# Three edits to a fused attention, SSM and mixture-of-experts kernel: the SSM's first batch begun inside the first FFN, another order at the start, a finer end

## The reference

```python
# attention (one head over 128 features)
q, k, v = jnp.split(jnp.einsum('bse,he->bsh', x, w_qkv), 3, axis=-1)
probs = jax.nn.softmax(jnp.einsum('bqh,bkh->bqk', q, k) * scale, axis=-1)
out = jnp.einsum('bqk,bkh->bqh', probs, v)        # then w_proj, b_proj
# SSM
zxbcdt = jnp.einsum('bld,ed->ble', u, W_in)       # z, xBC, dt
dt = jax.nn.softplus(dt + dt_bias)
conv = conv_b                                     # 4 taps along the tokens
for w in range(4):
    conv = conv + xp[:, w:w + L, :] * conv_w[:, w]
xBC = jax.nn.silu(conv)                           # x, B, C
def step(h, inp):                                 # scan over the tokens
    h = h * dA_t[:, :, None, None] + jnp.einsum('bhp,bn->bhpn', dtx_t, B_t)
    y_t = jnp.einsum('bhpn,bn->bhp', h, C_t)
g = y * jax.nn.silu(z)                            # RMS norm, then W_out
# FFN: 16 experts, the best 4 of each token by a router (softmax of logits)
# per expert: swiglu(mlp1_w[e] @ t + b1) -> mlp2_w[e], weighted sum
```

## Time and profile before

| | |
|---|---|
| timed executions | 749.07, 747.16, 748.96 us |
| the profiled execution | 746.62 us, of it the span 744.9 us |
| PE busy | 712.4 us (96%) |
| DVE busy | 627.3 us (84%) |
| ACT busy | 577.0 us (77%) |
| GpSimd (POOL) busy | 239.7 us (32%) |
| first FFN on PE | about 124 to 320 us |
| SSM, with its first batch's projections | about 320 to 555 us |
| second FFN on PE | about 555 to 740 us |

### The profile page before, as it was taken

One profiled execution on the slowest core, in us unless ns is written; L12 is line 12 of the kernel. 1 busy time (PEld: TensorE's weight loads), 2 busy tenths in 40 slices (PEclk: granted clock), 3 DMA queues, 4 the chain that ended last, 5 costly groups with the idle time before them and its releaser, 6 DMA issues. The chain is left out here.

```text
span 744.9 us, 13019 instructions
## 1 busy us (share of the span) xinstructions
PE 712.4 (96%) x3800; PEld 577.7 (78%) x3800; DVE 627.3 (84%) x1498; ACT 577.0 (77%) x1096; POOL 239.7 (32%) x389
## 2 busy tenths in 40 slices
PE   4999999999999999978999999999989999999997
PEld 3678788788788878757888888888768887887885
DVE  3568887999899899856779999899869999988986
ACT  2667677988988888847787787787668889888884
POOL 2336455000015010005677677677650000500000
PEclk9999999999999999999999999999999999999999
DMA  9000011645465555200000000000036455655661
GB/s 270 2 2 4 4 37 60 227 181 175 170 200 179 176 171 204 86 0 1 2 1 2 4 3 2 9 3 2 31 140 207 176 202 186 206 184 173 222 202 39
DMA packets 29237, 77.19 MB, mean 104 GB/s; under 512 B 4884, under 2 KB 9455, under 8 KB 29167
## 3 DMA queue, kind: packets, MB, share of 16 engines
q1 hardware_dynamic: 29012, 76.36, 30.6%
q10 hardware_dynamic: 154, 0.00, 0.0%
HBM read 73.73 MB, written 2.62 MB: 102 GB/s over the span
## 5 line engine op out<-in xcount | busy, mean ns | idle before, releaser
L684 ACT ACTIVATE s_ring<-ps,b1T 128x512 f32<-128x512 f32 x256 | 172.6, 690 | 37.8 <-PE ps L1591 36.6
L1110 DVE SCALAR_TENSOR_TENSOR s_ring<-s_ring,top_col,r_all 128x1024 f32<-128x1024 f32 x128 | 165.3, 1292 | 23.7 <-ACT s_ring L684 22.6
L1117 DVE TENSOR_TENSOR s_lo<-s_ring,s_hi 128x1024 fp32r<-128x1024 f32 x128 | 156.2, 1220 | 3.0 <-ACT s_hi L690 3.0
L690 ACT ACTIVATE s_hi<-s_ring 128x1024 fp32r<-128x1024 f32 x128 | 135.1, 1056 | 8.0 <-DVE s_ring L1110 7.5
L1565 PE MATMUL ps<-s_hi,w_hi 128*128 128x512 f32 x256 | 102.0, 399 | 2.8 <-DVE s_lo L1117 2.8
L1589 PE MATMUL ps<-ffn_hi,w_hi 128*128 128x512 f32 x256 | 103.9, 406 | 0.0
L1567 PE MATMUL ps<-s_hi,w_lo 128*128 128x512 f32 x256 | 101.3, 396 | 0.0
L1566 PE MATMUL ps<-s_lo,w_hi 128*128 128x512 f32 x256 | 101.2, 395 | 0.0
L1591 PE MATMUL ps<-ffn_hi,w_lo 128*128 128x512 f32 x256 | 101.1, 395 | 0.0
L1590 PE MATMUL ps<-ffn_lo,w_hi 128*128 128x512 f32 x256 | 101.1, 395 | 0.0
L1565 PEld LDWEIGHTS ps<-s_hi,w_hi 128*128 128x128 f32 x256 | 48.1, 188 | 17.4 <-DVE s_lo L1117 6.1
(11 more groups left out here) (232 smaller groups left out, 1552.2 us busy)
## 6 DMA issues: line engine op xcount, KB each, us to landing
r_all<-route_dram SPq DMA_DIRECT2D x128, 512.0 KB, 4.0
out_dram<-X SPq DMA_DIRECT2D x8, 256.0 KB, 4.4
X<-in_L_attn_a_x_dram SPq DMA_DIRECT2D x1, 1536.0 KB, 10.1
rows_f<-route_dram SPq DMA_DIRECT2D x48, 32.0 KB, 2.9
w_rows<-in_L_ffn_mlp_w_dram SPq DMA_DIRECT2D x1, 1024.0 KB, 6.4
route_dram<-route_cols SPq DMA_DIRECT2D x64, 8.0 KB, 1.5
X<-in_L_attn_a_x_dram SPq DMA_DIRECT2D x2, 256.0 KB, 3.0
in_rows<-in_L_attn_b_W_in_dram SPq DMA_DIRECT2D x1, 384.0 KB
```

The lines of the kernel that those rows point to most:

```text
L684: eng.activation(s_ring[q % NR][:, e % 2, :], bank(e % 4), ACT.Silu, bias=b1T[:, e:e + 1], scale=ALPHA).then_inc(F["act"], 1)
L690: eng.activation(s_hi[q % NR][:, :, :], s_ring[q % NR][:, :, :], ACT.Copy).then_inc(F["hi"], 1)
L1110: eng.scalar_tensor_tensor(out=s_ring[q % NR][:, :, :], in0=s_ring[q % NR][:, :, :], scalar=top_col[:, 0:1], in1=r_all[q % NR][:, :, :], o ...
L1117: eng.tensor_tensor(s_lo[q % NR][:, :, :], s_ring[q % NR][:, :, :], s_hi[q % NR][:, :, :].bitcast(F32), ALU.subtract).then_inc(F["lo"], 1)
```

## The change

1. **SSM's first batch inside the first FFN.** `late_router` of PE, ACT and DVE issues batch 0's projections between pairs of `F1`: statistics at (b, q) = (2, 5), normalisation (3, 3), `u_turn` (3, 7), `u_out` (4, 0), `u_low` (4, 1), the four `z_proj` at (4, 3), (4, 6), (5, 1), (5, 4) and their `z_out` a pair later, `dt_arg` (6, 0), `dt_exp` (6, 2), `softplus` in two parts at (6, 5) and (7, 1), `z_silu` (6, 6), `project_in` (7, 4) and (7, 5), `conv_first` (7, 7). The first conv tile stands between the last three `ffn_out` of the tail; the second conv tile stays behind the tail, with the two `seg_sum` of the scan ahead of it. The buffers of the early batch are freed places: parts of `ffn_hi` and `ffn_lo` of batches 0 and 1 hold its `u`, the rows of the SSM weights hold its `z`. The wait for the last `add_sum` moves from ahead of the scan to just before `y_skip`.
2. **Attention's first step in its own order.** `step(-1)` of attention does `xn_turn`, `q_proj` first, then the first four experts' weights, `v_proj`, then the next four, which go through bank 5.
3. **The end by halves.** In batch 7 of `F2` the low parts of the last two pairs are made expert by expert and waited for so; the sum is copied, turned, added and stored in two halves.

The buffers of the early batch:

```diff
+        early_zs = ssm_rows[:, 0:NT * (DI + NH)].rearrange("p (c e) -> p c e", c=NT)
+        early_uT = [t[:, 0:2, :].rearrange("p b t -> p (b t)")[:, 0:PAD + SEQ] for t in (ffn_hi, ffn_lo)]
```

ACT, in `late_router`:

```diff
+                if F is F1 and (b, q) == (NB - 1, 7):
+                    conv_first(0, 0)
+                    conv_first(0, 1)
+                if F is F1 and (b, q) == (NB, 2):
+                    conv_out(0)
...
+                elif F is F1 and (b, q) == (4, 0):
+                    u_out(0)
+                elif F is F1 and (b, q) in ((4, 4), (4, 7), (5, 2), (5, 5)):
+                    z_out(0, 0, ((4, 4), (4, 7), (5, 2), (5, 5)).index((b, q)))
+                elif F is F1 and (b, q) == (6, 2):
+                    dt_exp(0)
+                elif F is F1 and (b, q) == (6, 6):
+                    z_silu(0, 0)
```

PE, attention's first step (ACT's alike):

```diff
+                if i == -1:
+                    xn_turn(0)
+                    q_proj(0, 0)
+                    prep(0, 0)
+                    v_proj(0, 0)
+                    prep(0, 1)
+                    return
```

DVE, in `late_router`, `ffn_all` and `split`:

```diff
+                elif F is F1 and (b, q) == (2, 5):
+                    ssm_stats(0)
+                elif F is F1 and (b, q) == (3, 3):
+                    ssm_xn(0)
+                elif F is F1 and (b, q) == (4, 1):
+                    u_low(0)
+                elif F is F1 and (b, q) == (6, 0):
+                    dt_arg(0, 0)
+                elif F is F1 and (b, q) == (6, 5):
+                    softplus(0, 0, 0)
+                elif F is F1 and (b, q) == (7, 1):
+                    softplus(0, 0, 1)
...
                 for b in range(NB):
-                    if F is F1 and b == 6:
-                        ssm_stats(0, early=True)
                     ffn(F, b, b == 0, after_pair=lambda q: late_router(R, F, b, q))
+                ffn(F, NB, False, True)
                 if F is F1:
-                    ssm_xn(0, early=True)
-                ffn(F, NB, False, True)
+                    for k in range(2):
+                        for shift in range(1, CONV_W):
+                            conv_tap(0, k, shift)
...
+                if F is F2 and b == NB - 1 and q >= NQ - 2:
+                    for k in range(2):
+                        eng.tensor_tensor(s_lo[q % NR][:, k, :], s_ring[q % NR][:, k, :], s_hi[q % NR][:, k, :].bitcast(F32),
+                                          ALU.subtract).then_inc(F["lo"], 1)
+                    return
```

PE, in `late_router`, `decay_sums` and the SSM's step:

```diff
+                elif F is F1 and (b, q) == (3, 7):
+                    u_turn(0)
+                elif F is F1 and (b, q) in ((4, 3), (4, 6), (5, 1), (5, 4)):
+                    z_proj(0, ((4, 3), (4, 6), (5, 1), (5, 4)).index((b, q)))
+                elif F is F1 and b == NB - 1 and q in (4, 5):
+                    project_in(0, q - 4)
+                elif F is F1 and b == NB and q < 2:
+                    conv(0, 0, q)
...
             def decay_sums(b, par):
                 wait(eng, M["a"], b + 1)
+                if b == 0:
+                    eng.wait_ge(M["conv"], 6)
...
+                if i == -1:
+                    seg_sum(0, 0)
+                    seg_sum(0, 1)
                 if first:
                     conv(i + 1, 1, 0)
```

More of the change, by code:

```diff
@@ L703, in ffn @@
                             eng.wait_ge(R["lg_ps"], NB)
-                        eng.activation(acc_sb[:, :], bank(6), ACT.Copy).then_inc(F["acc_sb"], 1)
+                        if F is F2 and tail:
+                            for half in range(2):
+                                at = slice(half * SEQ // 2, (half + 1) * SEQ // 2)
+                                eng.activation(acc_sb[:, at], bank(6)[:, at], ACT.Copy).then_inc(F["acc_sb"], 1)
+                        else:
+                            eng.activation(acc_sb[:, :], bank(6), ACT.Copy).then_inc(F["acc_sb"], 1)
                     if not tail and (b, q) != (0, 0):
@@ L817, in conv_out @@
[L817 to L829, removed]
@@ new lines, in conv_tap @@
+            def conv_tap(b, k, s):
+                j = DVE_TILES[k]
+                if s == 1:
+                    wait(eng, M["tap"], 2 * b + k + 1)
+                else:
+                    wait(eng, M["conv"], 6 * b + 3 * k + s - 1)
+                eng.scalar_tensor_tensor(out=conv_acc[:, j, s:], in0=bank(7 - k if b else 5 - k)[:, 0:SEQ - s],
+                                         scalar=conv_taps[:, j, CONV_W - 1 - s:CONV_W - s], in1=conv_acc[:, j, s:],
+                                         op0=ALU.mult, op1=ALU.add).then_inc(M["conv"], 1)
@@ L1371, in step @@
                     cb_out(i, 0)
-                if first:
+                if first and i >= 0:
                     ssm_xn(i + 1)
@@ L1430, in step @@
                     weigh(F2, 0, 0)
-            skewed(eng, step, before={0: lambda: add_sum(F1, NB - 1, 0)})
+            skewed(eng, step, before={0: lambda: add_sum(F1, NB - 1, 3)})
             ffn_all(R2, F2)
-            add_sum(F2, NB - 1, 0)
+            for half in range(2):
+                wait(eng, F2["back"], 2 * NB + half)
+                rows = slice(2 * half, 2 * half + 2)
+                eng.tensor_tensor(X[:, NB - 1, rows, :], bank(half)[:, 0:2 * P].rearrange("p (r d) -> p r d", r=2),
+                                  X[:, NB - 1, rows, :], ALU.add).then_inc(F2["x"], 1)
         @block.tensor
@@ L1606, in ffn, with product, parts_of, u_of @@
                         after_pair(q)
+            def product(out, w, a, first=True, last=True):
+                eng.matmul(out, w[0], a[0], start=first, stop=False)
+                eng.matmul(out, w[0], a[1], start=False, stop=False)
+                return eng.matmul(out, w[1], a[0], start=False, stop=last)
+            def parts_of(t, *at):
+                return t[(slice(None), 0, *at)], t[(slice(None), 1, *at)]
+            def u_of(b, at):
+                return [part[:, at] for part in u_parts(b)]
@@ L1841, in step @@
                     cb_of(i, odd, 0)
+                if second and i > 0:
                     seg_sum(i, 0)
```

424 lines of the change are left out of this document (239 added, 185 removed).

## The result

The changed kernel takes 738.6 us (median of four runs, 737.45 to 739.27) where the kernel before takes 748.06 on the same chip: ratio 0.9881 with a 95% interval of 0.9861 to 0.9901. The forecast was 742.5 with a range from 739.5 to 746.0, so the direction was right and the size was not: it is 3.9 us too high, and the time lies under the range. Set against the kernel before, 8.9 us came off (by the ratio) where 5.9 were forecast. The profiled execution took 737.45 with a span of 735.7, 9.2 less than the 744.9 of before.

A forecast was written before the change was run, and what follows sets the result against it. The prediction took TensorE (PE), busy 96% of the span, as the bound. Its terms -1.9 + 3.8 + 2.5 - 10.5 + 1.2 - 1.0 = -5.9 us, from the mean 748.4, gave 742.5, range 739.5 to 746.0.

The forecast's parts named there:

- The base: Starting time of the sum: mean 748.4 us of three timed runs, about 2 above the profiled execution's 746.6.
- What DVE and ACT now do in the first FFN: First FFN: work moved onto DVE and ACT makes new stalls of PE, +2.5 us, ends 0 and 6.
- my places for new stalls: First FFN: exponential in batch 6, 1.0; softplus's second part, 1.0; batches 3 and 4, 1.0; stall at 278.14 gone, -0.5.
- PE's moved work: First FFN: turn, four z and two input projection products shift its end by +3.8 us, ends 3.4 and 4.2.
- The passage: From the first FFN's tail to the last sum's add: 21.6 us becomes 11.1, so -10.5.
- What is late next: From the add, the chain to the second batch's turn stays as before, 4.7 us, with PE idle 3.4.
- The clock: Behind PE's idle before the second batch's turn, the clock falls to 1.2 GHz: +1.2 us, ends 0 and 1.7.
- Rival (a): Passage to the SSM: the clock doesn't fall, -7.1 us, 741.3; chance 0.28.
- The end: Kernel's end: smaller low parts and overlapping halves of copy, turn, add and store, -1.0 us, ends -0.5 and -1.4.
- Attention: Attention's first step: the new order brings the first scores earlier, gain 1.6 to 2.1 us, taken as 1.9.
- (b): First FFN: moved work on DVE mostly uncovered, stalls 5 to 6 us, total -2.9, 745.5; chance 0.17.
- (c): First FFN: ACT and DVE alternate without overlap, stalls 11.8 us, total +3.4, 751.8, slower; chance 0.05.

The follow-up runs named there:

- x_pad: Changed kernel with one unused tile of 32 bytes per partition in front of each stage's own tiles: ratio 0.9881 to the kernel before.
- x_exp: Changed kernel with the exponential of dt in batch 6 of the first FFN one pair later on ACT: ratio 0.9878 to the kernel before.
- x_pe: Changed kernel whose early input projections of the first batch (four z, two conv inputs) take one matmul of three: median 736.4 us.
- x_dve1: Changed kernel with four unread statistics of 128 columns added on DVE at pair 4 of batches 3 to 7 of the first FFN: median 741.0 us.
- x_dve2: Changed kernel with eight unread DVE statistics per batch in batches 3 to 7 of the first FFN, four each at pairs 2 and 6: median 743.0 us.
- x_pool: Changed kernel with POOL's weighing and ramps of the first batch held back until DVE has normalised the second batch: median 735.8 us.
- x_clk: Changed kernel with 18 unread matmuls of 512 columns in PE's idle before the second batch's turn: median 736.1 us.
- x_best: Changed kernel with the last sum's turn earlier, POOL waiting for the normalisation and the exponential of dt one pair later: 733.62 us.

## Why the prediction was wrong

**The base, 0.65 us of the 3.9.** The sum was made on the profiled execution (740.7) and then moved up by 1.8 to the mean of the timed runs. By their times, two of those three runs were of the group with the lower clock in the passage, and this passage is what the change takes out. The changed kernel's median lies 1.15 above its own profiled execution (738.6 against 737.45), so 0.65 of the 1.8 was too much. The other 3.25, 740.7 against 737.45, is in the terms.

**The terms.** By the table the sum was too high by 3.7 in the first FFN, 0.6 in the second, 0.4 in attention, 0.3 in the clock and 0.1 at the end, and too low by 1.75 in the chain behind the add and 0.06 ahead of it. The chain's loss hid part of the first FFN's error: without it the miss would have been over 5.

**What DVE and ACT now do in the first FFN: the step that failed.** The term of +2.5 for new stalls rested on DVE's room: "in batches 3 to 7 where each leaves about 1.0" was read off one stretch of 14 us with DVE busy 13.41. The row is a load, not a capacity. The same stretch in the timeline of DVE, before:

```profile
286.13 1.28 DVE L1110 SCALAR_TENSOR_TENSOR s_ring<-s_ring,top_col,r_all 128x1024 f32<-128x1024 f32 x1
288.46 1.28 DVE L1110 SCALAR_TENSOR_TENSOR s_ring<-s_ring,top_col,r_all 128x1024 f32<-128x1024 f32 x1
...
293.81 1.29 DVE L1110 SCALAR_TENSOR_TENSOR s_ring<-s_ring,top_col,r_all 128x1024 f32<-128x1024 f32 x1 [0.38 <-ACT s_ring L684]
```

Up to 291 DVE makes up for the batch's own work ahead of these pairs (the sum at 285.53 among it), at 2.33 us a pair; then it waits for ACT, at PE's pace of 2.80. Over 140 to 154, with no stall of PE ahead of it in the FFN, it is busy just as long, and over 292 to 306 only 12.55:

```profile
140.00:154.00 14.00, 14.00 (x62) 11.26 (x61) 13.41 (x14) 12.46 (x17) 0.00 (x0) 1.00 0.61 220
```

So a pair of experts costs DVE 2.33 us when it runs freely and PE 2.80, and eight pairs leave 3.8, less 1.4 for the low rows and the sum: an estimate of 2.4 per batch where no router work stands, and low parts run ahead of PE besides. Against +3.8 for PE's work and +2.5 for stalls the first FFN grew by 2.56, and by 3.11 at the same pace (x_pad). The stalls there, waits with their slow first matmul, are 0.17, 0.27 and 1.17 in the changed kernel, 0.09, 0.20 and 1.15 in x_pad, and 0.11, 0.90 and 0.52 in the kernel before. That is +0.1 net in the changed kernel and -0.1 in x_pad, at the low end of 0 to 6 that I had weighted too little. Of my places for new stalls only the exponential of batch 6 came true, 1.17 in place of 1.0. The stall at the old place of the statistics did go, as x_exp shows. The one of 0.90 at 266.22 shrank to 0.27, because PE's own new work gives DVE time there: with part of that work left out, in x_pe, it is 0.72. **PE's moved work** is then 3.11 + 0.1 = 3.2, not 3.8: a busy time of a stretch with waits in it was a bad measure of it. x_exp, x_dve1 and x_dve2 show where the room does end: in batches 5 to 7.

**The passage: right.** -10.5 was forecast, -10.44 came. The taps were indeed done in time.

**What is late next: wrong by 1.75.** "Is as before, 4.7 us" counted instructions and not what else runs at the time. Before, POOL's weighing and ramps came behind the normalisation; moving the first batch's steps ahead put them beside it. The trace of before had a case of it, a product of two SBUF tiles that takes 0.69 elsewhere, beside POOL's second ramp and the weighing behind it:

```profile
344.27 1.52 DVE L1322 TENSOR_TENSOR gram<-segs,cb 128x512 f32<-128x512 f32 x1
```

The Trainium skill (SBUF — State Buffer, SBUF: two separate sides) states that DVE and GpSimd share a port pair under an exclusive lock, which the one that starts first holds for its whole instruction; on DVE's side it concerns an instruction in a mode that uses both ports, or one with two SBUF inputs against a GpSimd instruction that reads SBUF. The trace agrees that one blocks the other for whole instructions: 2.99 against 1.11 (x_pool), with each blocked normalisation ending 0.08 behind an operation of POOL. Who comes first it doesn't bear out by the recorded starts: the first normalisation is recorded at 330.79, 0.03 ahead of POOL's weighing, and ends behind it. It speaks against this change, and the prediction did not weigh it.

**The clock: right in kind.** It fell, at a price of 1.7 (x_clk; 1.5 to 2.6 over the traces) in place of 1.2. Set against before it shows as +0.87 only, since x_clk's stretch is 0.79 shorter than before's for reasons that no run isolates. Rival (a) is out.

**The end: right,** -1.06 against -1.0. **Attention: too small,** 2.5 against 1.9: the second weight set came 0.5 sooner behind v, and the third 0.4 sooner behind the second, than the old distances said. The constants, 0.77 later than before, took some of it back.

**What no step had.** The new tiles of the SSM in the common part moved the FFN's rings by 736 bytes, and that gave 0.55 in the first and 0.61 in the second FFN.

Rivals (b) and (c) are refuted: the moved work was mostly covered.

Open: why the place of a tile changes PE's pace, which tile it is, and what decides in which runs the clock falls in the passage.

## What to carry over

Take an engine's room from the free-running distance between its instructions, not from a busy share: a share near 1 over a short stretch may be an engine making up for what stood just before. The distance counts for added work too: four statistics of 0.28 each took 0.79. Where a step is moved, look at what the other engines do beside it in the new place, SBUF to SBUF work of DVE beside POOL above all. When a chain across engines ends the passage, its first link goes ahead of any work that could fill the idle behind it: the turn put ahead of 2.8 us of conv brought 4.3 us, of which part is that POOL no longer stood beside the normalisation.

## What the hardware showed that was not expected

Two kinds of DVE work on SBUF alone were held up beside POOL here, and one that reads PSUM was not: the normalisation 1.11 to 2.99; a product of two SBUF tiles 0.69 to 1.51 beside POOL's second ramp in x_best, while the low part of u, with one input in PSUM, kept its 0.68 beside the first:

```profile
332.32 0.68 DVE L1233 TENSOR_TENSOR uT<-ps,uT 128x512 fp32r<-128x512 f32 x1
332.91 1.51 DVE L1402 TENSOR_TENSOR gram<-segs,cb 128x512 f32<-128x512 f32 x1
```

PE's pace in a stream of matmuls hung on 32 bytes in the place of tiles (every tile of the stage moved with the rings, so it isn't shown that it is the rings): with the first ring at 157248 or 158016 within the partition a batch took 22.64 us, with 157280 or 157984 it took 22.50 to 22.54.
